# Key weight parts kept in DRAM and reloaded, and a new order of VectorE's work, in a rotary cross attention

## The reference, cut to what matters

```python
ctx = layer_norm(context, ln_ctx_g, ln_ctx_b)          # 2 x 2048 rows of 512
q = (lat @ Wq)                                         # 16 heads of 64
k, v = split(ctx @ Wkv)                                # 1024 columns of keys, 1024 of values
k = apply_rope(k, cos, sin)                            # x1*cos - x2*sin, x2*cos + x1*sin
attn = softmax(clip(q @ k^T / 8, -11, 11))
out = (attn @ v) @ Wo + bo
x = x + out
```

## Time and profile before

| | |
|---|---|
| median of 3 runs | 1240.84 us (1236.12 to 1246.4) |
| the profiled execution | 1246.6 us, span 1244.8 us |
| part of the span in which steps `t` run | about 28 us to 568 us |
| TensorE busy | 1172.4 us, 94% |
| VectorE busy | 839.5 us, 67% |
| ScalarE busy | 568.9 us, 46% |
| GpSimd busy | 275.2 us, 22% |
| mean granted TensorE clock | 0.971 |

### The profile page before, as it was taken

One profiled execution on the slowest core, in us unless ns is written; L12 is line 12 of the kernel. 1 busy time (PEld: TensorE's weight loads), 2 busy tenths in 40 slices (PEclk: granted clock), 3 DMA queues, 4 the chain that ended last, 5 costly groups with the idle time before them and its releaser, 6 DMA issues.

```text
span 1244.8 us, 23553 instructions
## 1 busy us (share of the span) xinstructions
PE 1172.4 (94%) x9792; PEld 959.9 (77%) x9792; DVE 839.5 (67%) x1377; ACT 568.9 (46%) x924; POOL 275.2 (22%) x184
## 2 busy tenths in 40 slices
PE   8698989798997989899999999999999999999998
PEld 6486868687786868785545667798889999999997
DVE  5949586777778594946678887346656565665663
ACT  5343332524343424311428999355644545444441
POOL 4226163645346362724000000001000000000000
PEclk9898999999898989899989999999899999999999
DMA  7112021203021210224631333320545444544440
GB/s 285 34 52 68 19 86 35 86 18 103 18 86 35 69 52 18 77 107 175 236 136 69 137 136 121 116 105 1 203 169 196 175 174 198 202 182 167 190 169 17
DMA packets 32192, 140.73 MB, mean 113 GB/s; under 512 B 3163, under 2 KB 3419, under 8 KB 21604
## 3 DMA queue, kind: packets, MB, share of 16 engines
q1 hardware_dynamic: 32100, 139.42, 30.3%
HBM read 138.88 MB, written 0.52 MB: 112 GB/s over the span
## 4 chain that ended last, share of the span: by engine, by line
PE 45%; DVE 3%; issue 2%; ACT 2%; DMA 1%; DVEq 0%; ACTq 0%
PE mid_bk L57 10%; PE mid_bk L58 10%; PE mid_bk L59 10%; PE mid_bk L1214 5%; PE mid_bk L1229 2%; PE mid_bk L1259 2%; PE mid_bk L1185 2%; PE mid_bk L1104 2%; PE mid_bk L1249 1%; DMA w_raw<-in_w 1%; PE mid_bk L1358 0%; DVE mo_w_lo L1891 0%; DVE mo_w_lo L1897 0%; ACT sa_sc L1524 0%; PE mid_bk L1310 0%
## 5 line engine op out<-in xcount | busy, mean ns | idle before, releaser
L626 POOL TENSOR_TENSOR norm_both<-norm_both,prob 128x512 f32<-128x512 f32 x118 | 190.1, 1611 | 87.5 <-DVE prob L400 80.1
L57 PE MATMUL k_ps<-ctx_hi,wk_hi 128*128 128x512 f32 x256 | 110.3, 431 | 47.3 <-DVE turned L380 46.5
L58 PE MATMUL mid_bk<-mo_x_lo,mo_w_hi 128*128 128x256 f32 x496 | 141.1, 284 | 0.0
L57 PE MATMUL mid_bk<-mo_x_hi,mo_w_hi 128*128 128x256 f32 x496 | 141.0, 284 | 0.0
L59 PE MATMUL mid_bk<-mo_x_hi,mo_w_lo 128*128 128x256 f32 x496 | 141.0, 284 | 0.0
L551 ACT ACTIVATE prob<-u_ps 128x512 f32<-128x512 f32 x128 | 66.0, 602 | 141.6 <-PE u_ps L773 141.6
L1897 DVE TENSOR_TENSOR mo_w_lo<-w_raw,mo_w_hi 128x2048 fp32r<-128x2048 f32 x32 | 73.3, 2292 | 74.4 <-ACT mo_w_hi L1606 74.4
L58 PE MATMUL k_ps<-ctx_lo,wk_hi 128*128 128x512 f32 x256 | 106.9, 417 | 0.0
L59 PE MATMUL k_ps<-ctx_hi,wk_lo 128*128 128x512 f32 x256 | 105.9, 414 | 0.0
L1606 ACT ACTIVATE mo_w_hi<-w_raw 128x2048 fp32r<-128x2048 f32 x32 | 61.2, 1913 | 91.1 <-PE mid_bk L59 91.1
L57 PE MATMUL mid_bk<-mo_w_hi,mo_h_hi 128*128 128x512 f32 x256 | 101.0, 394 | 0.0
(11 more groups left out here) (279 smaller groups left out, 2608.6 us busy)
## 6 DMA issues: line engine op xcount, KB each, us to landing
w_raw<-in_w SPq DMA_DIRECT2D x64, 1024.0 KB, 6.3
wk_raw<-in_wk_rows SPq DMA_DIRECT2D x32, 512.0 KB, 3.3
ctx_raw<-in_ctx_rows SPq DMA_DIRECT2D x8, 1024.0 KB, 5.5
x_k<-in_ctx_T SPq DMA_DIRECT2D x8, 1024.0 KB, 7.5
x_val<-in_ctx_heads SPq DMA_DIRECT2D x8, 1024.0 KB, 4.9
tabs<-in_rot_tabs SPq DMA_DIRECT2D x8, 512.0 KB, 3.3
vals<-in_wq_rows SPq DMA_DIRECT2D x4, 512.0 KB, 7.4
wv_raw<-in_wv_rows SPq DMA_DIRECT2D x4, 512.0 KB, 12.2
```

The lines of the kernel that those rows point to most:

```text
L57: pe.matmul(out, w_hi, x_hi, start=start, stop=False)
L58: pe.matmul(out, w_hi, x_lo, start=False, stop=False)
L626: ins = pool.tensor_tensor(to, to, src, ALU.add)
```

## The change

What moves, in three parts. First, the split of the key weights is done for steps 0 to 3 only; each pair of parts is written once to a DRAM tensor `wk_parts` (4 x 1 MB), and from step 4 on SyncE loads both parts (2 x 512 KB) straight into `wk_hi` and `wk_lo`, so that `project` waits for the DMAs and no longer for VectorE. Second, on VectorE `turn_first` and `turn_second` of a step come ahead of `sums`; `sums(n+1)` now stands in step `4n+3`, behind the turn and ahead of `clip`. Third, `stats` moves from step `4n+3` to step `4(n+1)`, and there `low_s` and `stats` now stand ahead of `clip`. On SyncE's queue the table load of a block moves ahead of the weight load of step `4n+1`. At the start, both first slices are split before the loop.

```diff
@@ load_wk(t), SyncE
                 if t >= 2:
                     sp.wait_ge(s["k_mm"], 2 * (t - 1))
-                sp.dma_start(wk_raw[:, t % 2, :, :], I["wk_rows"][g * P:(g + 1) * P, :]
-                             .rearrange("p (k n) -> p k n", k=KD)).then_inc(s_wk[t % 2], 16)
+                    if t != 3:
+                        sp.wait_ge(s["wk_kept"], 64 if t == 2 else 128)
+                if t < 4:
+                    sp.dma_start(wk_raw[:, t % 2, :, :], I["wk_rows"][g * P:(g + 1) * P, :]
+                                 .rearrange("p (k n) -> p k n", k=KD)).then_inc(s_wk[t % 2], 16)
+                    return
+                for half, part_of in ((0, wk_hi), (1024, wk_lo)):
+                    sp.dma_start(part_of[:, t % 2, :, :].bitcast(F32), I["wk_parts"][g * P:(g + 1) * P, half:half + 1024]
+                                 .rearrange("p (k n) -> p k n", k=KD)).then_inc(s_wk[t % 2], 16)
+
+            def keep_wk(t):
+                sp.wait_ge(s["wk_lo"], t + 1)
+                for half, part_of in ((0, wk_hi), (1024, wk_lo)):
+                    sp.dma_start(I["wk_parts"][t * P:(t + 1) * P, half:half + 1024].rearrange("p (k n) -> p k n", k=KD),
+                                 part_of[:, t % 2, :, :].bitcast(F32)).then_inc(s["wk_kept"], 16)
...
@@ SyncE's program
+            keep_wk(0)
+            keep_wk(1)
             for t in range(1, NT):
                 n, r = t // 4, t % 4
+                if r == 0:
+                    load_tab(n)
                 if t + 1 < NT:
                     load_wk(t + 1)
-                if r == 0:
-                    load_tab(n)
+                if t < 3:
+                    keep_wk(t + 1)
...
@@ VectorE's program
             low_k(0)
+            low_k(1)
             for t in range(NT + 1):
                 n, r = t // 4, t % 4
                 if t < NT:
-                    if r == 0:
-                        sums(n)
+                    if t in (1, 2):
+                        low_k(t + 1)
                     if r == 2 and n + 1 < NC:
                         center(dve, n + 1)
-                    if t + 1 < NT:
-                        low_k(t + 1)
                     turn_first(t)
                     if r == 2:
                         add_products(n, 1)
                     turn_second(t)
-                    if r == 3 and n + 2 < NC:
-                        stats(dve, n + 2)
+                    if t == 0:
+                        sums(0)
+                    if r == 3 and n + 1 < NC:
+                        sums(n + 1)
+                    if r == 0:
+                        if t == 0:
+                            for j in range(NWD):
+                                low_v(j)
+                        low_s(n)
+                        if n + 1 < NC:
+                            stats(dve, n + 1)
                 if t >= 1:
                     clip(t - 1)
                 if t < NT:
-                    if t == 0:
-                        for j in range(NWD):
-                            low_v(j)
-                    if r == 0:
-                        low_s(n)
-                        if t == 0:
-                            stats(dve, 1)
-                        if n + 1 < NC:
-                            spread(dve, n + 1)
+                    if r == 0 and n + 1 < NC:
+                        spread(dve, n + 1)
...
@@ project(t, a), TensorE
-                    pe.wait_ge(s["wk_lo"], t + 1)
+                    if t < 4:
+                        pe.wait_ge(s["wk_lo"], t + 1)
+                    else:
+                        pe.wait_ge(s_wk[t % 2], 32 * (t // 2))
```

More of the change, by code:

```diff
@@ L173, in cross_attention_rotary @@
                  "c_step", "c_var", "c_std", "ctp", "cfull", "csplit", "part_sum", "part_hi", "part_lo",
-                 "wk_hi", "wk_lo", "v_mm", "v_kept", "v_sum",
+                 "wk_hi", "wk_lo", "wk_kept", "v_mm", "v_kept", "v_sum",
                  "k_mm", "rope", "score", "exped", "clipped",
@@ L566, in _ @@
             queries(2)
+            high_k(1)
             high_v("B11")
             high_v("B21")
+            queries(3)
             high_v("B22")
-            queries(3)
             for t in range(NT + 1):
@@ L2169 @@
     out = nc.dram_tensor("out_x", (2, 128, 512), F32, kind="ExternalOutput").ap()
+    aps["wk_parts"] = nc.dram_tensor("wk_parts", (4 * 128, 2048), F32, kind="Internal").ap()
     program(nc, aps, out)
```

## The result

The changed kernel takes 1193.55 us (median of 4 runs, 1191.16 to 1195.95), beside 1241.43 us for the kernel before in the same comparison: ratio 0.9615, 95% interval 0.957 to 0.9659. The forecast was 1190. The profiled execution has a span of 1194.2 us, 50.6 less than before.

A forecast was written before the change was run, and what follows sets the result against it. TensorE, busy 94% of the span, was held at each block by VectorE's chain. Stalls 38.6, lower clock 15.4 and first block 2, less new waits 5.0, save 51.0 us: 1240.84 to 1190 us, range 1179 to 1211.

The forecast's parts named there:

- The stall and its clock: At seven block boundaries, TensorE's waits for the turn (38.6 us) and the lower clock behind them (15.4 us) go.
- The chain at block 2: VectorE's reordered work ends `turn_first(8)` at 171.0, 2.8 us before TensorE wants it; `clip(7)` ends at 181.9.
- The new waits: TensorE's `weigh` waits for `clip`: 0.4 us at four boundaries, 1.7 at blocks 3 and 5, 5.0 us in all.
- the wait moves to `clip`: Rival, chance 0.18: waits at `clip` of 2.6 us, 3.9 at two boundaries, with some lower clock: 1206 us.
- the upper bound of 2.6 us: Wait at `clip` if all sums took 1.43 us and both `low_s` operations 2.29 us.
- the swing of the clock from frequent short waits: Mechanism within the `clip` rival: every new wait costs 1.5 us at the lower clock; 1215 us with the longer waits.
- The other rule cited: VectorE's two-SBUF-input operations and GpSimd's SBUF reads exclude each other: sums take 2.3 us, boundary waits grow about 2.2.
- The date behind it: After `clip`, VectorE finishes the second sum of products at 189.9, TensorE wants it at 190.6: covered by 0.7 us.
- The loads: Weight DMAs of step 4n+1 land at 172.3, wanted by `project(9)` at 173.8: covered by 1.5 us, no cost.
- The first block: The 7.92 us wait before step 1 goes, mostly to no end: gain 2 us, bounds 0 and 7.9.
- The sum: Whole kernel: 38.6 + 15.4 + 2 - 5.0 = 51.0 us saved, forecast 1190 us.

The follow-up runs named there:

- the late load: Changed kernel with the weight load of step 4n+1 held back until the first half of step 4n's turn is done: 1231.85 us.
- The run with small additions: Kernel before with GpSimd's additions for the denominators cut to 2 of 128 columns, a probe that leaves out most sums of weights: 1192.77 us.
- Clip first: Changed kernel with `clip` ahead of `low_s` and the statistics in step 4n: 1195.15 us.
- the run with the statistics moved: Changed kernel with the next block's statistics and spread moved to step 4n+1 and the centring to step 4n+2: 1183.35 us.
- the two runs with `clip` first: `clip` ahead of `low_s` and statistics: on the changed kernel, 1195.15 us; on the kernel before with VectorE's new order and all splits, 1221.29 us.
- The repeat: Changed kernel measured once more, unaltered, on the chip of the three runs beside it: 1193.7 us.
- the order alone: Kernel before with VectorE's new order, key weights still split in every step: 1216.48 us.
- the parts alone: Changed kernel with VectorE's and SyncE's old order, key weight parts still loaded from DRAM: 1196.81 us.
- order and late statistics: Kernel before with VectorE's new order and statistics moved to step 4n+1, splits in every step, nothing kept in DRAM: 1201.9 us.

## Why the prediction was right, point by point

**The stall and its clock** (38.6 + 15.4): right, 54.0 against the 54.6 worked out above. All seven waits for the turn are gone and so is the lower clock behind them; the late load brings the stall back at seven boundaries and the lower clock at five.

**The chain at block 2**: right to a few tenths. From the last key matmul the end of the rotation took 3.5 us (3.56 predicted), the sums 4.9 (4.6), `clip` 1.4, rotation 3.8 behind its first half (3.56), `low_s` 3.4 (3.5). The new wait was 0.71 us (0.4). The run with small additions shows that the part put down to GpSimd, read from operations beside it and alone, was the right one: it adds 5.1 us to the chain, about the size of the stall.

**The new waits**: 5.0 predicted in six, 4.6 measured in five: none at block 1, 0.71 at blocks 2, 4 and 6, 1.69 at block 3 (1.7 predicted), 0.81 at block 5 (1.7), none at block 7. That the total is so close is in part luck. At block 3 the bias pair took 2.37 us beside GpSimd and not the 1.28 of the sum, but `low_s` took 2.35 and not 3.5. At blocks 1 and 5 GpSimd begins its work on a set of weights with a copy of 0.61 to 1.01 us in place of an addition, and the sums took 3.96 us and `low_s` 2.35: the prediction had priced every boundary by block 2. The rival "the wait moves to `clip`" had the place right and the size wrong. So the upper bound of 2.6 us for a wait at `clip` and the swing of the clock from frequent short waits did not come. The rule cited from the Trainium skill, TensorE: Matmul & The Clock Gate, "A second HAM failure mode: psum-queue depth-cycling", is not seen here, where five waits of 0.7 to 1.7 us left the clock at 1.00 from 100 to 520 us. The other rule cited, from the Trainium skill, SBUF — State Buffer, "Who interferes with whom", agrees with the runs in that operations with two SBUF inputs are slowed beside GpSimd (the run with small additions halves the sums' time), but the sums waited less than a whole addition each: 1.43 us and not 2.3. `clip` has one SBUF input and is slowed as well, which the rule as the prediction tells it doesn't cover.

**The date behind it**: "covered by 0.7" was wrong by 1.4. Clip first shows the second sum of products late by 0.67 us when the wait for `clip` is taken away. The term that was mis-sized is `spread`, put at 0.5 us. It took 1.2 us at this place in the kernel before and takes 1.4 in the changed one, most of it in its second operation, which begins beside GpSimd's additions. In the kernel before:

```profile
185.33 0.85 DVE L307 TENSOR_SCALAR cva<-cmv 128x4 f32<-128x4 f32 x1
```

In the changed kernel:

```profile
174.84 1.05 DVE L324 TENSOR_SCALAR cva<-cmv 128x4 f32<-128x4 f32 x1
```

The 0.5 would fit this operation away from GpSimd (0.17 us in the run with the statistics moved). The mis-sized term is 0.9 of the 1.4. In the changed kernel most of the lateness was hidden behind the wait for `clip`, but not all. VectorE is done at 183.59, and the matmul at 183.65 starts 0.45 us behind the one in front of it, where 0.23 is usual. Such a boundary costs 1.1 us with a listed wait of 0.71 (step 9 takes 20.4 us, and 19.3 in the run with the statistics moved). Over the layer the new waits cost 6.4 us (475.4 against 469.0), not the 4.6 listed and not the 5.0 predicted. The forecast suffered little; the expectations of the two runs with `clip` first failed by it.

**The loads**: right that they cost nothing, with more cover than said. The last of three DMAs was issued at 157.16 and landed at most 5.9 us later, by 163.1, where `project(9)` wanted it at 166.1: covered by 3.0 us, not 1.5. It was issued 8.9 us ahead of that date, and the sum had 9.2. From the tables' issue (156.31) to the last landing it took at most 6.8 us, and the sum had 8.4. A single load took longer than the 3.3 us of the sum (5.1 at the median for the second of a pair), but the three added less to each other than the 2.2 us each that the sum gave them. The queue's order had no effect.

**The first block**: 2 predicted, 1.4 found, and lost in a later start of the same size. The repeat doesn't have the late start, and gains 1.0. Writing the parts held back only SyncE (6.0 us in two waits) and neither ScalarE nor TensorE.

**The sum**: 51.0 predicted, 47.9 by the medians. Stalls and clock gave 54.6, the new waits took 6.4 and the first block with its late start took 0.4; that is the 47.8 of the layer. The forecast credited both halves of the change together, and didn't say what each is worth. The runs do: 25 us for the order alone, 44 for the parts alone, 48 for both.

## What to carry to other kernels

Where one engine must get through a run of items between two dates of the bottleneck engine, add up the whole run, to the last date: moving one item ahead moves the wait to another (clip first: nothing gained), while taking 3 us of work out to a place where the engine waits anyway gained 10, 6 of it at these dates. Read each duration beside and away from the engine that it shares with; here the sharing added 5.1 us to a chain that came 5.4 us too late, and making GpSimd's operations small gave as much as the whole change. Small operations count too: one of 128x4 elements took 0.17 us alone and 1.05 beside GpSimd. If a wait must remain, short ones can spare the lower clock that follows a long one; it did so here, but in the first block the waits grew by as much.

## What the runs showed of the hardware

- VectorE's operations with two SBUF inputs, and `clip` with one, slow down beside GpSimd's additions of 128x512: 1.43 against 0.71 us for a sum, 2.29 against 1.23 for `low_k`, up to 3.62 against 1.41 for four of `clip`. The statistics, with one SBUF input, took 2.46 us in every case, also at block 2 of the kernel before, where GpSimd adds during half of it.
- Which waits of TensorE were followed by the lower clock: over the boundaries of these profiles none of up to 2.2 us, all of 3.6 us and more, and in between some. Waits of 2.85 and 2.87 us were, in the run with the order alone, and one of 2.84 was not. At block 3 a wait of 3.51 us was not in that run, and one of 3.52 was in the run with order and late statistics. So the length of the wait alone doesn't decide it.
- A 512 KB write from SBUF to DRAM landed in 2.6 us (first of a pair) and 3.9 us (second), by the medians of four each in the changed kernel, about as long as loads of that size took alone, 3.3 us.
